# Loading the adjacency matrix by row groups, reloading x in pieces, and a shorter finish in a two-layer graph kernel

## The reference

```python
def _artan_k(x):  return jnp.arctanh(jnp.clip(x, -1.0 + 1e-07, 1.0 - 1e-07))      # KAPPA = -1, so sc = 1
def _tan_k(x):    return jnp.tanh(x)
def mobius_scalar_mul(r, x):
    x_norm = _norm(x)
    return _tan_k(r * _artan_k(x_norm)) * (x / x_norm)
def weighted_midpoint_lincomb(A, X):
    gamma = jnp.maximum(2.0 / (1.0 - jnp.sum(X * X, axis=-1, keepdims=True)), 1e-15)
    denom = _clamp_abs(A @ (gamma - 1.0))
    nom = A @ (gamma * X)
    two_mean = nom / denom
    sq = jnp.sum(two_mean * two_mean, axis=-1, keepdims=True)
    a_mean = two_mean / (1.0 + jnp.sqrt(jnp.maximum(1.0 - sq, EPS)))
    alpha = jnp.sum(A, axis=-1, keepdims=True)
    return mobius_scalar_mul(alpha, a_mean)
def logmap0(x):   xn = _norm(x); return _artan_k(xn) * x / xn
def expmap0(u):   un = _norm(u); return _tan_k(un) * u / un
# layer 2
XW = mobius_matvec(W, X)
AXW = weighted_midpoint_lincomb(A_hat, XW)
return expmap0(jax.nn.relu(logmap0(AXW)))
# the whole: h = relu(layernorm(x)); x = x + attention(h, adj, adj, ...); h = relu(layernorm(x)); x = x + layer2(h, adj, W)
```

## Time and profile before

| | |
|---|---|
| device time, median of 3 runs | 861.0 us (859.3 to 863.12) |
| the profiled execution's own time | 860.4 us |
| its span in the profile | 858.6 us |
| PE busy | 754.5 us (88%) |
| DVE busy | 664.4 us (77%) |
| ACT busy | 491.3 us (57%) |
| POOL busy | 47.7 us (6%) |
| read from HBM, written | 148.16 MB, 8.42 MB |

### The profile page before, as it was taken

How to read it: one execution, slowest core, us unless ns; L and a number is a source line. 1 busy time by engine, 2 the same in 40 slices (tenths; PEclk the granted TensorE clock), 3 DMA queues, 4 the chain that set the end, 5 groups by cost and what they waited for, 6 DMA issues and landing times.

```text
span 858.6 us, 15125 instructions
## 1 busy us (share of the span) xinstructions
PE 754.5 (88%) x4989; PEld 693.8 (81%) x4996; DVE 664.4 (77%) x1370; ACT 491.3 (57%) x897; POOL 47.7 (6%) x96
## 2 busy tenths in 40 slices
PE   5999789999999999994665889999999999999780
PEld 4888677787778888783565889999999999999780
DVE  6778668878877888775585568888888888888865
ACT  2444366677776777676562335555555555555774
POOL 0000011000101000000000000000000000000340
PEclk9999989999999999998786999999999999999995
DMA  5115376776677776635409989999899889989631
GB/s 136 50 57 214 134 283 228 287 286 230 229 259 255 279 287 235 227 103 120 95 1 219 245 182 199 184 185 186 179 183 184 180 179 180 181 178 186 134 113 49
DMA packets 53373, 157.13 MB, mean 183 GB/s; under 512 B 9040, under 2 KB 30800, under 8 KB 47184
## 3 DMA queue, kind: packets, MB, share of 16 engines
q1 hardware_dynamic: 53328, 156.60, 68.8%
HBM read 148.16 MB, written 8.42 MB: 182 GB/s over the span
## 4 chain that ended last, share of the span: by engine, by line
PE 62%; DVE 15%; DMA 7%; SPq 4%; issue 4%; ACT 4%; DVEq 3%; ACTq 0%
PE bank L591 47%; PE bank L702 8%; DMA adjL<-in_adj 3%; DVE least L1420 3%; DMA adjU<-in_adj 2%; DVE adjT_lo L1360 2%; SPq L419 2%; PE bank L688 2%; PE bank L657 2%; DVE least L1404 2%; SPq L483 1%; DVE X_lo L1338 1%; DVE bank L1352 1%; DVE v L1221 1%; PE bank L583 1%
## 5 line engine op out<-in xcount | busy, mean ns | idle before, releaser
L591 PE MATMUL bank<-X_hi,adjT_hi 128*128 128x258 f32 x1024 | 296.1, 289 | 36.6 <-DVE adjT_lo L1360 36.6
L591 PE MATMUL bank<-X_hi,adjT_lo 128*128 128x258 f32 x1024 | 294.1, 287 | 0.0
L591 PE MATMUL bank<-X_lo,adjT_hi 128*128 128x258 f32 x1024 | 294.0, 287 | 0.0
L591 PEld LDWEIGHTS bank<-X_hi,adjT_hi 128*128 128x128 f32 x1024 | 198.9, 194 | 39.4 <-DVE adjT_lo L1360 26.2
L591 PEld LDWEIGHTS bank<-X_lo,adjT_hi 128*128 128x128 f32 x1024 | 199.4, 195 | 0.0
L591 PEld LDWEIGHTS bank<-X_hi,adjT_lo 128*128 128x128 f32 x1024 | 199.0, 194 | 0.0
L909 ACT CAST adjT_hi<-bank 128x1024 fp32r<-128x1024 f32 x96 | 97.4, 1014 | 131.5 <-PE bank L591 88.5
L1352 DVE STREAM_TRANSPOSE bank<-adjL 128x1024 f32<-128x1024 f32 x96 | 119.6, 1246 | 36.2 <-DMA adjL<-in_adj 36.1
L1360 DVE TENSOR_TENSOR adjT_lo<-bank,adjT_hi 128x1024 fp32r<-128x1024 f32 x96 | 116.1, 1210 | 16.7 <-ACT adjT_hi L909 16.4
L702 PE MATMUL bank<-values,probT 128*128 128x256 f32 x512 | 121.2, 381 | 4.9 <-ACT probT L945 4.8
L702 PEld LDWEIGHTS bank<-values,probT 128*128 128x128 f32 x512 | 93.2, 190 | 18.7 <-ACT probT L945 7.2
(11 more groups left out here) (168 smaller groups left out, 1119.8 us busy)
## 6 DMA issues: line engine op xcount, KB each, us to landing
adjL<-in_adj SPq DMA_DIRECT2D x128, 512.0 KB, 9.1
adjU<-in_adj SPq DMA_DIRECT2D x32, 1024.0 KB, 5.7
adjL<-in_adj SPq DMA_DIRECT2D x16, 2048.0 KB, 10.0
x_scratch<-x SPq DMA_DIRECT2D x16, 258.0 KB, 3.5
xin<-in_x SPq DMA_DIRECT2D x8, 512.0 KB, 3.8
xt<-in_x SPq DMA_DIRECT2D x16, 256.0 KB, 3.3
x_all<-x_scratch SPq DMA_DIRECT2D x4, 1024.0 KB, 17.6
out_x<-res SPq DMA_DIRECT2D x8, 512.0 KB, 2.9
```

The source lines that it names most:

```text
L591: last = pe.matmul(dst, a[i][a_cols], b[j][b_cols], start=(k_first and n == 0), stop=(k_last and n == 2))
```

## The change

Three things change.

1. The four transfers of a tile are cut in another way. Before, transfer a brought column quarter a of all 128 rows, to the 32 partitions a*32 to a*32 + 31. Now transfer i brings the 32 whole rows 32i to 32i + 31 to all 128 partitions. What lies where in `adjL` afterwards is the same, and so are the bytes and the length of each contiguous piece (4 KB). Before, both sides of a transfer counted 32 x 4 x 1024 elements. Now the source counts 4 x 32 x 1024 (quarters, rows, columns) and the destination 128 x 1024.
2. `x1_all` comes back in 16 transfers of 256 KB in place of 4 of 1 MB: one behind each of tiles 2 and 3, then one behind each pair of tiles.
3. The finish leaves out the first tanh and the second log with its series. In their place the argument is held below `FURTHEST`, the arctanh of 1 - 2^-23. The two parts `finish_product` and `finish_log` and one `finish_series` go.

```diff
+FURTHEST = math.atanh(1.0 - 2.0 ** -23)
-FINISH_FUNCTIONS = [(ACT.Sqrt, "squares", "roots"), (ACT.Ln, 5, 5), (ACT.Tanh, 2, 2), (ACT.Ln, 5, 5),
-                    (ACT.Tanh, 1, 3)]
-FINISH_CHUNKS = (1, 2, 4, 5, 7)
+FINISH_FUNCTIONS = [(ACT.Sqrt, "squares", "roots"), (ACT.Ln, 5, 5), (ACT.Tanh, 1, 3)]
+FINISH_CHUNKS = (1, 2, 4)
...
-    adj_q = adj.rearrange("(t s r) (a f) -> t a r s f", s=QD, r=RB, a=QD)
+    adj_q = adj.rearrange("(t s r) (a f) -> t s a r f", s=QD, r=RB, a=QD)
...
             def mean_adj(t, par):
-                for a in range(QD):
-                    sp.dma_start(adjL_q[a * RB:(a + 1) * RB, par], adj_q[t, a]).then_inc(d_adj[par], 16)
+                for i in range(QD):
+                    sp.dma_start(adjL_q[:, par, i], adj_q[t, i]).then_inc(d_adj[par], 16)
...
+            def x1_back(i):
+                sp.dma_start(x1_all_2[:, i], x1_pairs[i]).then_inc(s_x1_all, 16)
+
             for t in range(2):
                 mean_adj_next(t, t)
-                for part in range(2 * t, 2 * t + 2):
-                    sp.dma_start(x1_all[:, part * HT // 2:(part + 1) * HT // 2, :],
-                                 x1_dram[part * N // 4:(part + 1) * N // 4, 0:D].rearrange("(t p) d -> p t d", p=P))\
-                      .then_inc(s_x1_all, 16)
+                x1_back(t)
+
             with sp.Fori(1, HT - 1) as i:
                 for par in range(2):
                     mean_adj_next(2 * i + par, par)
+                x1_back(i + 1)
...
-            dve.wait_ge(s_x1_all, 16 * 4)
+            dve.wait_ge(s_x1_all, 16 * HT)
...
             def finish_scaled(c):
                 artanh_end(V[2][:, c], V[5][:, c], V[6][:, c], V[7][:, c])
-                tt(V[2][:, c], V[2][:, c], alpha[:, c], ALU.mult).then_inc(s_f, 1)
-            def finish_product(c):
...
-            def finish_log(c):
-                artanh_end(V[2][:, c], V[5][:, c], V[6][:, c], V[7][:, c])
-                tt(V[0][:, c], V[0][:, c], V[2][:, c], ALU.mult)
+                tt(V[2][:, c], V[2][:, c], alpha[:, c], ALU.mult)
+                dve.drain()
+                dve.scalar_tensor_tensor(out=V[0][:, c], in0=V[2][:, c], scalar=FURTHEST, in1=V[0][:, c], op0=ALU.min,
+                                         op1=ALU.mult)
                 dve.drain()
                 tt(V[1][:, c], V[0][:, c], roots[:, 2, c], ALU.mult)
...
-            FINISH_PARTS = (finish_root, finish_mean, finish_series, finish_scaled, finish_product, finish_series,
-                            finish_log, finish_exp)
+            FINISH_PARTS = (finish_root, finish_mean, finish_series, finish_scaled, finish_exp)
```

More of the change, by code:

```diff
@@ L1 @@
+import math
 import concourse.bass as bass
@@ L98, in graph_layers_kernel @@
         x1_dram = nc.dram_tensor("x1_scratch", [N, XW], F32, kind="Internal").ap()
+        x1_pairs = x1_dram.rearrange("(i j p) d -> i p j d", j=2, p=P)[:, :, :, 0:D]
         x1_halves = x1_dram.rearrange("(h s p) d -> s p h d", p=P, h=2)
@@ L216, in graph_layers_kernel @@
         x1_all = place("x1_all", [P, T, D], "qx")
+        x1_all_2 = x1_all[:, :, :].rearrange("p (i j) d -> p i j d", j=2)
         qx_v = qx[:, :, :].rearrange("p (g j) c -> p g j c", j=BPC)
@@ L549, in _ @@
                 steps(pool, pair)
-            pool.wait_ge(s_x1_all, 16 * 4)
+            pool.wait_ge(s_x1_all, 16 * HT)
             for t in range(FIRST_BATCH):
@@ L1559, in finish_scaled @@
                 artanh_end(V[2][:, c], V[5][:, c], V[6][:, c], V[7][:, c])
-                tt(V[2][:, c], V[2][:, c], alpha[:, c], ALU.mult).then_inc(s_f, 1)
-            def finish_product(c):
-                function_done()
-                tt(V[0][:, c], V[0][:, c], V[2][:, c], ALU.mult)
+                tt(V[2][:, c], V[2][:, c], alpha[:, c], ALU.mult)
                 dve.drain()
[L1567 to L1572, removed]
-            def finish_log(c):
-                artanh_end(V[2][:, c], V[5][:, c], V[6][:, c], V[7][:, c])
-                tt(V[0][:, c], V[0][:, c], V[2][:, c], ALU.mult)
+                dve.scalar_tensor_tensor(out=V[0][:, c], in0=V[2][:, c], scalar=FURTHEST, in1=V[0][:, c], op0=ALU.min,
+                                         op1=ALU.mult)
                 dve.drain()
```

## The result

The changed kernel takes 1140.4 us (median of 4 runs, 1138.95 to 1141.02) where the kernel before takes 860.2 on the same chips. The ratio is 1.325, with a 95% interval of 1.321 to 1.329. The forecast was 1144 us, in a range from 1090 to 1500.

What follows compares the result with a forecast made beforehand. PE was taken to bound most of the kernel before, transfers the mean after: tile 2 issued at 460.7, 630 us for 30 tiles, 12.0 for x, 1.6 start and landing, 18.9 twice, 1.8 around: 1144 us, range 1090 to 1500.

Steps and rivals of the forecast that it cites:

- The step that decided: Transfers of adj in the mean: 4 outermost at the source gives four shares, so four engines for all of a tile.
- The rate: Tile transfers in the mean: four engines take 21.0 us a tile, between 19.5 and 24.1, against PE's 11.4.
- The surcharge: Tile transfers: 20.2 us raised to 21.0, since engines will sometimes meet at the same place in SBUF.
- the straight line: Time of a 4 KB piece, drawn between 8 KB and 1 KB pieces: 0.158 us, 25.9 GB/s, 20.2 us a tile.
- The port rival: Tile transfers: four engines write in step to the same SBUF ports, 42 us a tile, 1816 us; chance 0.07.
- its milder form: Tile transfers: four engines in step part of the time, 25 to 38 us a tile, 1270 to 1690 us; chance 0.13.
- The beginning: First tiles of the mean: tile 0 lands near 405, tile 1 at 427.0, tile 2 is issued at 460.7 us.
- The end: After tile 31: 18.9 us to the last copy of a mean, then 18.9 in place of 23.7 to the end.
- the sum: Whole kernel: tile 31 at 1104.3 plus 18.9 and 18.9 gives 1142.1 us of span, with 1.8 around it 1144.
- The rival with 16 engines: Tile transfers: all 16 engines work, each spread over 128 partitions, 4.9 us a tile, 837 us; chance 0.13.

Runs made afterwards that it cites:

- number 5: Changed kernel with each transfer of a tile halved into two column quarters of 32 rows, eight transfers a tile: 1788.4 us, ratio 2.078.
- number 6: Changed kernel with each transfer of a tile cut in four, one column quarter of 32 rows each, sixteen transfers a tile: 841.1 us, ratio 0.977.
- number 1: Kernel before with the new cut of a tile alone; x in four transfers and the long finish stay: 1143.0 us, ratio 1.328.
- number 8: Changed kernel with x back in four transfers of 1 MB; new cut and short finish stay: 1139.5 us, ratio 1.323 to the kernel before.
- number 9: Changed kernel with the old cut, and the 16 pieces of x behind tiles 2 to 17, one a tile: 839.8 us, ratio 0.976.
- number 7: Changed kernel with sixteen one-quarter transfers a tile, column quarters in the order 0, 2, 1, 3: 837.7 us, ratio 0.973.
- number 12: Changed kernel with the old cut, four transfers a tile, column quarters in the order 0, 2, 1, 3: 846.7 us, ratio 0.982.

## Why the prediction was right

**The step that decided** was the number of shares. The trace of before could not show it, since all its large transfers have a multiple of 16 outermost. It held: 4 outermost, four small packets and some four engines; 2 outermost, two and half the rate (number 5); 32, sixteen (number 6). This is what the Trainium skill's page "DMA: Bandwidth & Descriptors" states in the section "Why a DMA increments its semaphore by 16 and not by 1", and the runs agree for 2, 4 and 16. What the runs don't show is which engines these are. Nor do they show the part of both sides: the destination has 128, 64 or 32 outermost in them, always a multiple of the source's count, so a rule that looks at the source alone would give the same.

**The rate** was 21.0 us a tile and is 20.4 without x (number 1), 20.98 with it. I had 21.4 with x. The surcharge that I put on the straight line for meetings in SBUF was too much. The line itself has a wrong point: the 26.9 GB/s between 120 and 122 us are not of 8 KB pieces. Its 52 packets carry 0.85 MB, 16 KB each. A line from 16 KB (0.609 us) to 1 KB (0.047) gives 0.159 us for 4 KB, 25.7 GB/s and 20.4 us, which is what was measured. For x I had 12.0 us in all; with 20.34 for a tile (27 of them in number 1, from 548.19 to 1097.35), 608.5 - 29 x 20.34 = 18.6 are left for it. The port rival is dead for this shape: its 42 us would need 50 GB/s, and its milder form 25 us at least. Number 5 has 52 from two engines that fill two quarters, 26 each.

**The beginning** was forecast some 5 us too early: tile 0 near 405 (407.77), tile 1 at 427.0 (432.06), tile 2 issued at 460.7 (465.76) and waited for until 490.24, 24.5 us after its issue where I had 22.6. I had 1.6 us for the start and the landing of a tile. SP needed 6.3 us for four issues that took 1.9, but that this is the delay isn't shown: tile 2's four issues took 4.55, and it came no sooner.

```profile
404.10 6.30 SPq L423 DMA_DIRECT2D adjL<-in_adj  x4
```

**The end** held in one part: from the last copy to the end 18.9 us were forecast and 18.9 measured (1120.29 to 1139.2). From tile 31 to the last copy it was 21.5 where I had 18.9. I had written that POOL's wait for x costs nothing, since its sums end before DVE's. They do, but they stand in DVE's way: 2.2 us of it go when x comes back in four transfers (number 8), and 6.3 where PE sets the pace (number 9).

Tile 31 came at 1098.76 where I had 1104.3. So the sum is 2.9 us too high in the span. That it is so near is luck in part, since errors of both signs cancel: tile 2 was issued 5.1 us later than forecast and took 1.9 longer, 29 tiles took 19.1 less, x took 6.6 more, and the end 2.6 more. What was not luck is the number of engines: it moves the time by hundreds of us, these errors by less than 20.

**The rival with 16 engines** gave 837 for the same edits without the loss. Sixteen shares by groups of rows measure 841.1, or 837.7 in the better order. They get there by another way than that rival's: no transfer of `adj` fills all 128 partitions there, and no run here shows what 16 engines make of one that does in the mean.

## What to carry to other kernels

Before a transfer is reshaped, write both sides as they are handed over, outermost count first. In the runs here the smaller of the two counts, up to 16, is how many engines work, however many partitions are touched: 4 in the changed kernel, 2 in number 5, 16 for 32 and for 128. Counts of which one doesn't divide the other were not run. When a stage waits for transfers at a DMA share of 0.3, count the small packets of a transfer before blaming bytes. And an operation off the critical path can still hold up one on it: look at what runs beside it, not only at when it ends.

## What the runs showed of the hardware that I had not expected

- Sixteen engines that all fill the same 32 partitions move 12.5 GB/s each. With 128 KB transfers in the order 0, 1, 2, 3 it is 15.4 (number 6), and 18.8 when they alternate between partitions 64 apart (number 7). With 512 KB ones in that second order it is 13.2 (number 12).
- One DVE subtraction took 6.00 us in place of 1.2 while POOL ran 24 sums without a gap, and five of DVE's 128 x 2 operations took 0.5 to 0.8 in place of 0.17 beside such a row, some with one input only (the changed kernel, 1103 to 1107 us).
- SP's issue of four such transfers took 6.4, 6.3 and 4.55 us for tiles 0, 1 and 2 in the changed kernel, against 1.9. Tile 3's four took 17.4, and a single piece of x behind tile 2 took 5.2, against 0.43 in number 6. In number 5 the first eight, half as large, took 26.1. So SP is held up by what stands in the queue. Whether that is all, or the shape's decoding costs too, the runs don't tell.
